# Latent attention with the softmax division moved behind the weighing, and a new order of work

## The reference

```
q = x @ Wq;  latent = x @ Wkv_down
k = latent @ Wk_up;  v = latent @ Wv_up
attn = softmax(where(mask, q k^T / 8, -inf))
y = attn @ v;   out = y @ Wout
```

## Time and profile before

| | us |
|---|---|
| median of 3 runs | 2306.94 (2294.31 to 2309.14) |
| profiled execution: its time | 2307.74 |
| profiled execution: span of the trace | 2305.5 |
| share of the span: PE, DVE, POOL, ACT | 89%, 74%, 66%, 57% |
| mean granted TensorE clock | 0.945 |

### The profile page before, as it was taken

The page is one execution under the profiler, slowest core; times in us unless marked ns, Lnnn a source line. Parts: engine busy times, 40 slices in busy tenths (PEclk is TensorE's granted clock), DMA queues, the critical chain, the costliest instruction groups (busy, mean ns, idle before and its releaser), DMA issues. The chain is left out here.

```text
span 2305.5 us, 45315 instructions
## 1 busy us (share of the span) xinstructions
PE 2047.1 (89%) x15360; PEld 1606.3 (70%) x15360; DVE 1714.5 (74%) x3132; ACT 1315.3 (57%) x3178; POOL 1532.9 (66%) x1401
## 2 busy tenths in 40 slices
PE   6579999999899999999998788979998989899985
PEld 4467777777677777777777576767676767677764
DVE  5587777677777887777676248888788788888883
ACT  3356566656665676567665356555655556456541
POOL 2465566556645755666465128988888789888984
PEclk7789999999999999999999889999999999999998
DMA  8343333333333333333333206777678767777685
GB/s 271 102 100 93 92 87 77 94 88 94 76 93 91 99 91 91 88 89 77 80 91 81 91 25 151 184 197 196 163 187 204 182 165 195 203 179 180 177 206 140
DMA packets 189280, 298.18 MB, mean 129 GB/s; under 512 B 52265, under 2 KB 97149, under 8 KB 188029
## 3 DMA queue, kind: packets, MB, share of 16 engines
q1 hardware_dynamic: 171388, 254.91, 43.1%
q10 hardware_dynamic: 10752, 21.51, 3.7%
q0 software_dynamic: 6912, 18.89, 3.2%
HBM read 56.04 MB, written 20.97 MB: 33 GB/s over the span
## 5 line engine op out<-in xcount | busy, mean ns | idle before, releaser
L2043 POOL TENSOR_TENSOR g_ring<-g_ring,g_rl 128x768 f32<-128x768 f32 (+6 forms) x168 | 384.8, 2304 | 40.7 <-DVE g_rl L1984 35.8
L1872 ACT ACTIVATE g_ring<-ps,g_mx 128x128 f32<-128x128 f32 (+7 forms) x384 | 274.2, 727 | 200.3 <-DVE g_mx L1966 92.2
L1759 PE MATMUL ps<-g_turned,g_latV 128*64 128x256 f32 (+1 forms) x1984 | 294.3, 442 | 73.6 <-issue 40.5
L855 ACT ACTIVATE l_pp<-ps,l_mx 128x256 f32<-128x256 f32 (+1 forms) x512 | 229.2, 464 | 169.0 <-DVE l_mx L992 169.0
L1131 POOL TENSOR_TENSOR l_pp<-l_pp,l_rl 128x1024 f32<-128x1024 f32 (+1 forms) x128 | 229.8, 1796 | 88.4 <-DVE l_rl L1000 88.2
L1991 DVE STREAM_TRANSPOSE g_ring<-g_ring 128x896 f32<-128x896 f32 (+4 forms) x264 | 257.2, 998 | 13.8 <-POOL g_ring L2043 13.5
L1759 PEld LDWEIGHTS ps<-g_turned,g_latV 128*64 128x64 f32 x1984 | 149.4, 143 | 162.9 <-issue 99.3
L1148 POOL TENSOR_TENSOR l_act_lo<-l_u,l_act_hi 114x512 fp32r<-114x512 f32 x96 | 125.5, 1307 | 162.4 <-ACT l_act_hi L905 162.2
L992 DVE CUSTOM_DVE_ANT_0 ps<-ps,l_mask 128x256 f32<-128x256 f32 (+1 forms) x512 | 188.4, 443 | 7.8 <-PE ps L704 7.8
L110 PE MATMUL ps<-l_wqkv_hi,l_x_hi 128*128 128x512 f32 x384 | 168.0, 437 | 17.9 <-POOL l_x_lo L1101 12.9
L110 PE MATMUL ps<-l_h_hi,l_w_hi 128*114 128x512 f32 (+1 forms) x384 | 160.7, 418 | 25.0 <-DVE l_h_lo L1049 22.2
(11 more groups left out here) (201 smaller groups left out, 6251.0 us busy)
## 6 DMA issues: line engine op xcount, KB each, us to landing
l_pt<-l_bt SPq DMA_DIRECT2D x1024, 64.0 KB, 2.0
g_turned<-g_ring SPq DMA_DIRECT2D x192, 112.0 KB, 3.0
g_turned<-g_ring SPq DMA_DIRECT2D x140, 128.0 KB, 3.8
g_turned<-g_pt SPq DMA_DIRECT2D x140, 128.0 KB, 3.5
g_turned<-g_ring SPq DMA_DIRECT2D x184, 96.0 KB, 2.9
g_turned<-g_ring SPq DMA_DIRECT2D x192, 80.0 KB, 2.4
g_turned<-g_pt SPq DMA_DIRECT2D x96, 96.0 KB, 2.2
l_tab<-turns SPq DMA_DIRECT2D x64, 128.0 KB, 2.1
```

Source lines behind the costliest of these rows:

```text
L855: act.activation(PP[:, i % NP, at, 0:n], ps[:, bank + a, jj * 2 * P:jj * 2 * P + n], ACT.Exp, bias=mx[:, g % 2, h, at:at + 1], scale=-1.0, ...
L1759: last = pe.matmul(o, latV[:, b % 2, c, :], turned[:, :, a, c, :, :], start=(c == 0), stop=(c == t), skip_group_check=True)
L1872: act.activation(to, some, ACT.Exp, bias=mx[:, u % 2, at:at + 1], accum_out=sm[:, u % 2, at:at + 1]).then_inc(s["ex"], 1)
L2043: pool.tensor_tensor(view, view, some, ALU.mult).then_inc(s["scaled"], 1)
```

## The change

The exponentials stay unnormalised: `scale` is gone, and `blocks` waits for the exponential alone. `share` takes the reciprocals of a whole unit at once (96 instead of 224). A new step on GpSimd, `spread`, repeats each head's reciprocal over 64 columns next to the place of the context in `g_ctxu`. At the start of `weigh` TensorE transposes these (`size/2` transposes of 128x128) into PSUM behind the context, `evacuate` copies both, and `divide` on GpSimd multiplies the context by the turned reciprocals before it splits it. For 8 heads the weighing thus takes two neighbouring banks. GpSimd issues 4 of a unit's 16 transfers, ScalarE 2, SyncE 10. `QS` goes from 5 to 4, `g_ctxu` doubles. All offsets and spacings of the plan, and some of its costs, are new.

```diff
-QS = 5
+QS = 4
-    ASIDE = (((0, 0), (1, 1), (2, 2)),) * LONG + (((0, 0), (1, 1)),) * (NT - LONG)
-    BELOW = (((3, 3), (0, 1)),) * LONG + (((2, 2), (3, 3)),) * (NT - LONG)
-    COST = (2.798, 3.485, 2.704, 3.109, 4.273, 4.971, 2.906, 5.516)
+    ASIDE = (((0, 0), (1, 1)),) * LONG + (((0, 0), (1, 1)),) * (NT - LONG)
+    BELOW = (((2, 2), (3, 3), (0, 1), (1, 2)),) * LONG + (((2, 2), (3, 3), (0, 1), (1, 2)),) * (NT - LONG)
+    COST = (3.461, 3.877, 2.618, 3.291, 5.131, 5.397, 2.083, 5.582)
...
-        "pool": {"split_x": -58.63, "scale": -23.93, "divide": 15.42, "move": -11.05},
+        "pool": {"split_x": -61.0, "spread": 29.32, "divide": -119.57, "move": 45.66},
...
+        if event[0] == "weigh" and self.size(event[1]) == 8:
+            runs = [r for r in ((i, i + 1) for i in range(7)) if late(r) is not None]
+            return min(runs, key=lambda r: (late(r), -r[0])) if runs else None
...
-        ctxu = sb("g_ctxu", [P, NCU, CH])
+        ctxu = sb("g_ctxu", [P, NCU, 2 * CH])
...
+                        pe.wait_ge(s["spread"], u + 1)
+                        n = plan.size(u) // 2
+                        for j in range(n, 2 * n):
+                            at = bank * CH + j * P
+                            pe.transpose(flat[:, at:at + P], ctxu[:, u % NCU, j * P:(j + 1) * P], ident[:, :])
...
-                        act.wait_ge(s["rl"], first[u - 1])
+                        act.wait_ge(s["rl"], u - 1)
...
-                    n = plan.size(u) // 2 * P
-                    act.activation(ctxu[:, u % NCU, 0:n], ps[:, bank, 0:n], ACT.Copy).then_inc(s["ev"], 1)
+                    n = plan.size(u) * P
+                    act.activation(ctxu[:, u % NCU, 0:n], flat[:, bank * CH:bank * CH + n], ACT.Copy).then_inc(s["ev"], 1)
...
-                def share(k):
-                    u, p = pairs[k]
-                    dve.wait_ge(s["ex"], heads[k + 1])
-                    if u >= 2 and p == 0:
-                        dve.wait_ge(s["scaled"], first[u - 1])
-                    own = slice(mine(k), mine(k) + plan.wide(units[u][1]))
+                def share(u):
+                    dve.wait_ge(s["ex"], heads[first[u + 1]])
+                    if u >= 2:
+                        dve.wait_ge(s["spread"], u - 1)
+                    own = slice(0, plan.size(u))
                     dve.reciprocal(rl[:, u % 2, own], sm[:, u % 2, own]).then_inc(s["rl"], 1)
...
-                    dve.wait_ge(s["scaled"], k + 1)
+                    dve.wait_ge(s["ex"], heads[k] + a + n)
...
-                def scale(k):
-                    u, p = pairs[k]
-                    pool.wait_ge(s["rl"], k + 1)
-                    n = plan.wide(units[u][1])
-                    view = probs(k, 0, n).rearrange("p j (a x) -> p a j x", a=n)
-                    some = rl[:, u % 2, mine(k):mine(k) + n].unsqueeze(2).unsqueeze(3).to_broadcast([P, n, 4, keys(u) // 4])
-                    pool.tensor_tensor(view, view, some, ALU.mult).then_inc(s["scaled"], 1)
+                def spread(u):
+                    pool.wait_ge(s["rl"], u + 1)
+                    if u >= NCU:
+                        pool.wait_ge(s["clo"], u - NCU + 1)
+                    if u == 0:
+                        pool.wait_ge(s["cut"], 4)
+                    n = plan.size(u)
+                    pool.tensor_copy(ctxu[:, u % NCU, n * DH:2 * n * DH].rearrange("p (h d) -> p h d", h=n),
+                                     rl[:, u % 2, 0:n].unsqueeze(2).to_broadcast([P, n, DH])).then_inc(s["spread"], 1)
...
                     view = ctxu[:, u % NCU, 0:n * P].rearrange("p (j q) -> p j q", j=n)
+                    part = ctxu[:, u % NCU, n * P:2 * n * P].rearrange("p (j q) -> p j q", j=n)
                     pool.wait_ge(s["ev"], u + 1)
+                    pool.tensor_tensor(view, view, part, ALU.mult).then_inc(s["scaled"], 1)
+                    pool.wait_ge(s["scaled"], u + 1)
                     if z:
                         pool.wait_ge(s["wo"], KD * z)
                     pool.tensor_copy(ch[:, j, tok], view).then_inc(s["chi"], 1)
```

More of the change, by code:

```diff
@@ L1226, in __init__ @@
         some = [(k, a) for k, a in heads if a == 0 or self.long(k)]
-        events = {"scores": [e for k in range(K) for e in self.steps(k)], "share": [("share", k) for k in range(K)],
-                  "exp": [("exp", k, a) for k, a in heads], "scale": [("scale", k) for k in range(K)],
+        events = {"scores": [e for k in range(K) for e in self.steps(k)], "share": [("share", u) for u in range(U)],
+                  "exp": [("exp", k, a) for k, a in heads],
                   "largest": [("largest", k, a) for k, a in apart], "blocks": [("blocks", k, a) for k, a in some],
@@ L1235, in __init__ @@
             events[kind] = [(kind, z) for z in range(Z)]
-        for kind in ("evacuate", "divide", "move"):
+        for kind in ("evacuate", "spread", "divide", "move"):
             events[kind] = [(kind, u) for u in range(U)]
@@ L1272, in rank @@
         at = self.RANK[engine][kind]
-        if kind in ("scores", "share", "exp", "scale", "largest", "blocks"):
+        if kind in ("scores", "exp", "largest", "blocks"):
             return self.start[n] + at
-        if kind in ("weigh", "evacuate", "divide", "move"):
+        if kind in ("share", "spread", "weigh", "evacuate", "divide", "move"):
             return self.start[self.first[n + 1] - 1] + at
@@ L1295, in cost @@
                 return 0.1 + heads / 2 * (0.18 + sum(3 * (c / 2400 + (0.018 if c > P else 0.056)) for c in parts))
-            return {"share": 0.12, "exp": 0.235 + 0.00084 * w, "scale": 0.06 + 0.00183 * w * heads}.get(
-                kind, 0.08 + 0.00104 * w * (1 if (self.apart(n) if kind == "largest" else self.long(n)) else heads))
+            if kind == "exp":
+                return 0.235 + 0.00084 * w
+            return 0.05 + 0.00107 * w * (1 if (self.apart(n) if kind == "largest" else self.long(n)) else heads)
+        if kind == "spread":
+            return 0.2 + 0.00085 * self.size(n) * DH
         if kind == "weigh":
@@ L1300, in cost @@
             some = 1 if t == 0 else (t + 2) // 2 if event[2] == 0 else t + 1 - (t + 2) // 2
[L1301 removed]
+            return 0.1 + some * (0.44 if t >= self.LONG else 0.91) + (0 if event[2] else 0.055 * self.size(n))
         if kind in ("evacuate", "divide"):
[L1303 removed]
+            return (0.00166 if engine == "act" else 0.0051) * self.size(n) * P / 2 + (0.15 if engine == "act" else 0.55)
         if kind == "move":
@@ L1336, in needs @@
                 if lead and event[2] == 0:
-                    out += [("dve", ("share", last))]
+                    out += [("dve", ("share", u - 2))]
                 if u >= SLOTS_G and p == 0 and event[2] == 0:
                     out += [(some, ("move", u - SLOTS_G)) for some in ("sp", "act", "pool")]
[L1340 to L1343, removed]
-            else:
-                out += [("pool", ("scale", n))]
+            else:
+                out += [("act", ("exp", n, event[2]) if self.long(n) else end(n))]
+        elif kind == "share":
+            k = self.first[n + 1] - 1
+            out += [("act", ("exp", k, self.wide(self.units[n][1]) - 1))] + ([("pool", ("spread", n - 2))] if n >= 2 else [])
+        elif kind == "spread":
+            out += [("dve", ("share", n))] + ([("pool", ("divide", n - 2))] if n >= 2 else [])
         elif kind == "move":
@@ L1351, in needs @@
             b, t, r = self.units[n]
-            out += [(some, ("move", n)) for some in ("sp", "act", "pool")] + [ ("act", ("values", (b * NT + t) // TZ))]
+            out += [(some, ("move", n)) for some in ("sp", "act", "pool")] + [ ("act", ("values", (b * NT + t) // TZ)), ("pool", ("spread", n))]
             ago = self.units[max(n - 2, 0)]
```

22 lines of the change are left out of this document (11 added, 11 removed).

## The result

The changed kernel takes 2348.48 us in the median of four runs (2329.49 to 2362.83), the kernel before 2308.04 beside it: ratio 1.0176, 95% interval 1.0144 to 1.0209. That is about 41 us slower, where 29 us faster was forecast, and outside the range. The profiled execution took 2356.19 us (span 2354.4), somewhat above its median, so of its trace I use stretches and shares.

The account below looks back on a forecast made before the run. Four queues at 83 to 90%, waiting for one another, TensorE fullest, were taken to bound it. -5.7 us per batch, -23 in four, -29 with the ends: 2307.7 becomes 2279, own range 2262 to 2298.

Parts of the forecast that it names:

- What bounds the kernel now: Latent attention body, 900 us: four queues at 83 to 90%, none at its limit, time made by waiting for one another.
- GpSimd: Body: 530.8 us of scalings removed, spreads, products and 192 issues added; busy time 768 becomes 460 us.
- SyncE: Queue of moves: 160 issues fewer, -115 us, 806 becomes 691; a unit of 4 heads waits 7.2 us instead of 8.6.
- ScalarE: Copies out of PSUM double in width: +27 us, hidden; if not, 0.2 to 0.5 us a unit.
- TensorE: 256 added transposes ahead of the weighing at 0.13 us each: +33 us, bounds 33 and 42, on the path.
- The product: 96 multiplications on GpSimd by the turned reciprocals: 80 us, or 88 at the upper row.
- The sum: Body by chunks: TensorE 95% full in tiles 0 to 5, 93% in 6 and 7; -5.7 us per batch, 2279.
- The one on the slower side, 2335 by banks: PSUM rival: waits for moves become waits for banks, 95 us idle stay, transposes on top: 2335 us; chance 17%.
- The transfers bound, no change: Rival: moves land no sooner though issued sooner, tiles 6 and 7 stay at 87: 2305, up to 2320; chance 20%.
- the rival of held issues: Each of GpSimd's 384 issues waits out a VectorE block turn of 1.2 us: 2342 us; chance 2%.
- The rule of the Trainium skill: GpSimd-issued transfers wait during two-port VectorE operations, about 3.1 us instead of 0.62: some 550 us slower; prediction said trace disagrees.
- The two ends: Kernel's end -4.3 us, start -1.7 us, from scalings and issues that go: together -6 us.

Follow-up runs that it names:

- b_half: Kernel before in its own order, each transfer of a move carrying half its columns (all but 5 of 96 units): 2272.12 us, ratio 0.9843.
- a_pool2: Changed kernel, same order, GpSimd issuing 2 of a unit's 16 transfers, ScalarE 2, SyncE 12: 2353.85 us, ratio 1.0198 to the kernel before.
- a_copy: Changed kernel without transposes and product, wide copies kept: 2311.39 us, ratio 1.001 to the kernel before.
- a_transposes: Changed kernel with its transposes, but without wide copies and product: 2331.91 us, ratio 1.0121 to the kernel before.
- b_noscale: Kernel before in its own order with GpSimd's scaling left out and nothing in its place: 2309.84 us, ratio 1.0005.
- a_bare: Changed kernel without transposes, wide copies and product, spreads kept: 2308.38 us, ratio 1.0002 to the kernel before.
- b_transposes: Kernel before with 256 identity transposes added ahead of the weighings, behind the waits for the moves: 2324.02 us, ratio 1.0064.

## Why the prediction was wrong

- **What bounds the kernel now: partly wrong.** I counted 806 us of issues on SyncE and read the queue as a partner near its limit. The count was right, for in the trace they add up to 802 us, but the reading was not. b_half shows a kernel 37 us faster with the same count, and so that the transfers' bytes weigh; a_pool2 shows that 192 issues can change place at no net cost. TensorE's waiting for landings was read rightly, its cause was not: I gave it to the issuing, and to GpSimd's scaling ahead of it.
- **GpSimd: the prices right, the worth wrong.** 460 us forecast, 467 measured (over 940 us). The worth of the relief is nothing, with whole and with half transfers. The wait behind the scaling that the chunks at 95% seemed to show was no wait that set the kernel's time. A likely reason, not tested, is that the probabilities had a place to stay (four buffers) while TensorE worked on older units.
- **SyncE: wrong.** 160 issues fewer were to save 115 us; they saved 32 (802 to 770 us in the traces), since each took longer. A unit's issues were to shrink from 8.6 to 7.2 us; in tiles 6 and 7 they take 9.0.
- **ScalarE: right.** +27 forecast, +27 in the groups, and a_copy shows them hidden.
- **TensorE: the mis-sized term.** 33 to 42 us forecast; 50.4 measured. I took the spacing inside a group of four, but 64 of the 96 groups are pairs, which take 0.44 us in the median, where the last one's drain is shared by two. On time they cost some 27 us (a_transposes).
- **The product** was priced on GpSimd's queue and then forgotten, since that queue was no bound. It stands between the weighing and all that follows, and costs about 14 us. By which wait is open; the wait for the spread is not it.
- **The sum: the step that failed.** "TensorE stays the fullest, its two partners near the limit are relieved, and what matters is how full TensorE gets": I let it go from 90.5% to some 94% (95% and, in tiles 6 and 7, 93%) and the clock return, -9 us of idle and +3 of busy time per batch. It was 91.8%, +13.2 busy and -2.2 idle, the clock 0.97 in that batch. The fill was assumed, with no row that said what would close the gaps: the relief that was to close them is worth 0.0% when it comes alone (b_noscale), and the gaps were TensorE's waits for landings, which halving the bytes shortens (b_half).
- **The rivals.** The one on the slower side, 2335 by banks, had the right sign and arithmetic (all idle time kept, the transposes on top), but not the shown mechanism: the holds of banks through wide copies cost nothing (a_copy), and a_bare keeps the banks at no cost. "The transfers bound, no change" named what TensorE waits for and then left the transposes out of tiles 6 and 7. GpSimd's 384 issues stayed at 0.50 us each, so the rival of held issues did not come about. The rule of the Trainium skill ("SBUF — State Buffer", section "SBUF: two separate sides") speaks of VectorE operations of the two-port kind. No run here shows that any of VectorE's was of that kind, so the trace does not test the rule, and the prediction's word that the trace disagrees with it goes too far.
- **The two ends: about right.** From the start of the last tiles 6 and 7 to the end of the span it took 117.5 us (2354.4 - 2236.9) against 120.5 before, though that holds a longer chunk.

## What to carry to other kernels

An engine at 85% is no reason to take work from it: leave the work out first, with nothing in its place, and see if the time moves. Here that one run says the relief is worth 0.0% (interval -0.3% to 0.2%), and the price that was paid for it, mostly on the fullest engine, was a loss. For a queue of transfers look at two lengths, the issue's own and the time from issue to landing: here halving the bytes left the median issue at 0.59 us, took the landing from 2.8 to 2.0 us and the kernel down by 37.

## What the runs showed of the hardware

- Identity transposes of 128x128 in single precision: 0.66 us for four in a row, but 0.44 in the median for two, and 50.4 us of busy time for 256.
- 256 of them cost 13 to 15 us in the kernel before, with 47.9 us of TensorE's busy time in its body (b_transposes), and some 27 us in the changed one.
- Halving the bytes of the moves' transfers took SyncE's median issue from 592 to 591 ns, and the median time from issue to landing from 2.8 to 2.0 us.
- In the same order of work SyncE's transfers land after 2.7 us in the median with 2 of a unit's 16 issued by GpSimd (a_pool2), and after 3.2 us with 4 (changed kernel). The kernels take the same time.
- With a third of the score products left out the granted clock of the batch was 0.95 instead of 0.98, between its levels of 2.4 and 1.2 GHz. That the saving caused this is not shown, as like batches of one trace (b_noscale) have 0.95 and 0.98 too.
